# The gates' chain moved into its PSUM bank, and the join of the key halves' maxima made a one-operand reduction

## The reference

```python
x = x + tanh(g_xattn) * xattn(layernorm(x), ctx)        # 8 heads of 64, softmax, Wo, bo
x = x + tanh(g_ffn) * ffn(layernorm(x))

# ffn: attention of x with itself, 16 heads of 32 (q normalised, scaled, biased), giving h; then
gates = softmax(h @ Wr.T + br)                          # 15 routed gates per token
routed = gates * (one-hot mask of the 3 largest) * 3
sw = softmax(h @ Ws.T + bs)                             # 2 per token
shared = sw; weight_0 = sw * 2
masked = concat([weight_0[..., 0:1] * shared, weight_0[..., 1:2] * routed])
out = (h * masked.sum(-1, keepdims=True)) @ Wp.T + bp
```

## Time and profile before

| | us |
|---|---|
| median of 3 runs (lowest, highest) | 5000.62 (4998.94, 5014.54) |
| span of the profiled execution (its own device time is not listed apart) | 5005.2 |
| TensorE busy in it | 4571.6 (91%) |
| VectorE busy | 3138.7 (63%) |
| ScalarE busy | 2516.0 (50%) |
| GpSimd busy | 3389.9 (68%) |
| mean granted TensorE clock | 0.956 of full speed |

### The profile page before, as it was taken

The page is one execution under the profiler, slowest core; times in us unless marked ns, Lnnn a source line. Parts: engine busy times, 40 slices in busy tenths (PEclk is TensorE's granted clock), DMA queues, the critical chain, the costliest instruction groups (busy, mean ns, idle before and its releaser), DMA issues.

```text
span 5005.2 us, 67480 instructions
## 1 busy us (share of the span) xinstructions
PE 4571.6 (91%) x21568; PEld 2352.4 (47%) x21568; DVE 3138.7 (63%) x3955; ACT 2516.0 (50%) x4577; POOL 3389.9 (68%) x2667
## 2 busy tenths in 40 slices
PE   4899999999999999998989989999999899899886
PEld 3455555545454545454444544544444445444333
DVE  4554545454545454576767777776767677777764
ACT  3343434353434343445656656556556566465453
POOL 1665656565656565566777778777778687777766
PEclk8999999999999999999999999999999999999988
DMA  7466565756555656554344344353434353443432
GB/s 227 123 175 176 154 189 154 202 154 179 143 166 145 174 144 164 145 141 133 96 120 125 98 128 131 87 148 112 131 104 121 102 142 91 126 123 96 126 87 72
DMA packets 516174, 682.50 MB, mean 136 GB/s; under 512 B 42609, under 2 KB 371825, under 8 KB 506609
## 3 DMA queue, kind: packets, MB, share of 16 engines
q1 hardware_dynamic: 515824, 678.18, 48.9%
HBM read 323.83 MB, written 150.99 MB: 95 GB/s over the span
## 4 chain that ended last, share of the span: by engine, by line
PE 73%; DVE 10%; DMA 7%; issue 4%; ACT 4%; SPq 2%; POOL 1%; ACTq 0%; DVEq 0%; POOLq 0%
PE aux L903 25%; PE aux L995 19%; PE aux L1009 17%; PE aux L977 6%; DVE nm L1333 3%; PE aux L1021 3%; DVE h_raw L1353 2%; DMA xs<-x_after_xattn 2%; ACT probs L1193 1%; SPq L792 1%; DMA xs<-in_x 1%; DMA x_after_xattn<-xs 1%; PE aux L947 1%; DMA raw<-in_ctxT 1%; PE aux L1029 1%
## 5 line engine op out<-in xcount | busy, mean ns | idle before, releaser
L882 POOL TENSOR_TENSOR added<-added,probs 128x512 f32<-128x512 f32 x1433 | 1828.5, 1307 | 904.2 <-PE aux L1009 517.3
L1333 DVE TENSOR_REDUCE nm<-aux 128x2 f32<-128x1024 f32 x1536 | 1809.9, 1220 | 908.4 <-PE aux L977 907.5
L1193 ACT ACTIVATE probs<-aux 128x512 f32<-128x512 f32 x2151 | 1186.5, 599 | 1086.8 <-PE aux L995 1047.3
L995 PE MATMUL aux<-stack 128*128 128x512 f32 x4096 | 1430.0, 441 | 145.9 <-ACT probs L1193 61.6
L995 PEld LDWEIGHTS aux<-stack 128*128 128x128 f32 x4096 | 721.3, 193 | 1003.3 <-issue 340.4
L1009 PE MATMUL aux<-probs,v 128*32 128x512 f32 (+1 forms) x4302 | 985.2, 628 | 2.4 <-ACT probs L1193 1.3
L882 POOL TENSOR_TENSOR added_f<-added_f,probs 128x512 f32<-128x512 f32 x537 | 679.5, 1301 | 124.3 <-PE aux L1009 104.3
L977 PE MATMUL aux<-ck_hi,cq_hi 32*128 32x512 f32 (+1 forms) x3072 | 466.8, 499 | 167.9 <-DVE nm L1333 133.9
L903 PE MATMUL aux<-xT_hi,wqk 128*128 128x512 f32 x1536 | 584.1, 424 | 3.7 <-ACT v_out L1163 1.6
L977 PEld LDWEIGHTS aux<-ck_hi,cq_hi 32*128 32x128 f32 (+1 forms) x3072 | 183.8, 191 | 631.9 <-issue 607.3
L903 PE MATMUL aux<-wvo,parts 128*128 128x512 f32 x1536 | 406.6, 402 | 13.4 <-issue 9.6
(11 more groups left out here) (128 smaller groups left out, 4535.1 us busy)
## 6 DMA issues: line engine op xcount, KB each, us to landing
wqk<-w_split SPq DMA_DIRECT2D x256, 256.0 KB, 3.8
wvo<-w_split SPq DMA_DIRECT2D x64, 1024.0 KB, 7.2
parts<-h_kept SPq DMA_DIRECT2D x128, 512.0 KB, 4.2
stack<-cq_hi SPq DMA_DIRECT2D x128, 256.0 KB, 6.0
stack<-ck_hi SPq DMA_DIRECT2D x128, 256.0 KB, 6.4
v_kept<-v_out SPq DMA_DIRECT2D x128, 256.0 KB, 2.5
v<-v_kept SPq DMA_DIRECT2D x64, 512.0 KB, 6.1
h_kept<-h_hi SPq DMA_DIRECT2D x128, 256.0 KB, 2.4
```

Source lines behind the costliest of these rows:

```text
L882: pool.tensor_tensor(onto, onto, exp_buffer(T, e), ALU.add).then_inc(added_ok, 1)
L995: ins = pe.matmul(out, stack[:, g % 2, e * ph.SLOTS + ks, jt * P:(jt + 1) * P], stack[:, g % 2, e * ph.SLOTS + qs, n * HALF:(n + 1) * HALF ...
L1193: act.activation(exp_buffer(T, e), aux[:, o.bank["S", T, e], :], ACT.Exp, scale=ph.SCALE).then_inc(probs_ok, 1)
L1333: dve.tensor_reduce(nm[:, half, first:first + 2 * TT - t:TT], aux[:, b:b + 2, :], axis=AX.X, op=ALU.max, negate=True).then_inc(emptied["dv ...
```

## The change

The chain of the gates is no longer one item `gm` but three, `gs` (VectorE, up to the subtractions), `ge` (ScalarE, the exponential) and `gm` (VectorE, the rest), with planned times of 1, 0.2 and 2.6 us in place of `ga`'s 0.2 and `gm`'s 4 us, and due steps right after `gt`. The last half's logits are added in the gates' own PSUM bank, subtracted and exponentiated there, and sums live there too, so that no instruction of the chain has two tensor operands in SBUF; the bank is freed by `gm` rather than by `ga`. `gexp` falls away. `mc` becomes a reduction over the two halves' columns of `nm` into a new tensor `least`, which `mt` transposes. In `run`, the held rule is lifted where nothing is under way.

```diff
--- before.py
+++ after.py
@@ -118,7 +118,7 @@
 
 
 BATCH_HAS = {kind: n for n, kinds in (
-    (1, ("cl", "xl", "cx", "cxl", "ln", "la", "lb", "l2", "tr", "tra", "trl", "wv", "wo", "xr")), (2, ("gm",)),
+    (1, ("cl", "xl", "cx", "cxl", "ln", "la", "lb", "l2", "tr", "tra", "trl", "wv", "wo", "xr")), (2, ("gs", "ge", "gm")),
     (NG, ("wl", "pq", "pk", "pqa", "pka", "pql", "pkl", "ss", "ssa", "s2", "s3", "s3p", "sd", "mx", "mxr", "mc", "mt", "ml", "md", "vl")),
     (TT, ("vp", "vpe", "vs", "ol", "op", "ope", "xb", "st", "xq")), (HALVES, ("sm", "sma", "ev", "acc", "gt", "ga", "hs", "hsl", "hw")),
     (TURN, ("S", "ex", "ad", "PV"))) for kind in kinds}
@@ -219,7 +219,13 @@
                 self.add(("ev", h), "dve", 2.07, b + 0.6, [("sma", h), ("PV", T), ("ev", h - 1), ("hw", h - 1)])
                 if ph.ffn:
                     self.add(("gt", h), "pe", 0.45, b + 1, [("ev", h), ("fb", 0)])
-                    self.add(("ga", h), "dve", 0.2, b + 1.2, [("gt", h), ("gm", 2 * (h // HALVES - 1) + h % 2)])
+                    if h // 2 % NG < NG - 1:
+                        self.add(("ga", h), "dve", 0.2, b + 1.2, [("gt", h)])
+                    else:
+                        part = 2 * (h // HALVES) + h % 2
+                        self.add(("gs", part), "dve", 1, b + 1.2, [("gt", h)])
+                        self.add(("ge", part), "act", 0.2, b + 1.3, [("gs", part)])
+                        self.add(("gm", part), "dve", 2.6, b + 1.4, [("ge", part), ("ope", TT * j - 1)])
                 self.add(("hs", h), "act", 0.55, b + 1, [("ev", h)])
                 self.add(("hsl", h), "dve", 0.6, b + 1.2, [("hs", h), ("gt", h)])
                 self.add(("hw", h), "sp", 1.3, b + 1.5, [("hsl", h)])
@@ -326,9 +332,6 @@
         last = [("vp", TT * (j + 2) - 1, whole - 1)] if j + 1 < 2 * B else [("op", TT * j - 1, NG - 1)]
         self.add(("wo", j), "sp", 1.3, b0 + at["out"][0] - 4, last + [("ws", ph.W + 3)])
         self.add(("xr", j), "sp", 2.6, b0 + at["xr"], [("tr", j + 1, 1, NG - 1), ("st", TT * j - 1), ("fs", NG * j + NG - 1)])
-        if ph.ffn:
-            for half in range(2):
-                self.add(("gm", 2 * j + half), "dve", 4, b0 + (2 if half else -4), [("ga", HALVES * (j + 1) - 2 + half), ("ope", TT * j - 1)])
         for i in range(TT):
             half, t = i // (TT // 2), TT * j + i
             b = b0 + at["out"][0] + at["out"][1] * i
@@ -379,7 +382,7 @@
                     engine, time, _ = work[it]
                     unit = Order.unit(it)
                     if it[0] in Order.TAKER and unit not in banks:
-                        if held and it[0] not in ("S", "PV", "sm", "gt"):
+                        if held and events and it[0] not in ("S", "PV", "sm", "gt"):
                             continue
                         b = some(it[0], 4 if it[0] == "mx" else 1)
                         if b is None:
@@ -467,6 +470,8 @@
             return [(("mxr", *unit[1:], p), banks[2 * p:2 * p + 2]) for p in range(2)]
         if unit[0] == "acc":
             return [(("ev", unit[1]), banks)]
+        if unit[0] == "gt" and unit[1] // 2 % NG == NG - 1:
+            return [(("gm", 2 * (unit[1] // HALVES) + unit[1] % 2), banks)]
         kind = "pqa" if unit[0] == "pq" and stage(batch(unit)).ffn else Order.TAKER[unit[0]]
         return [((kind,) + unit[1:], banks)]
 
@@ -498,10 +503,10 @@
         xs = sb("xs", [P, TT // 2, DM])
         xT_hi = sb("xT_hi", [P, NG, N], F32R)
         xT_lo = sb("xT_lo", [P, NG, N], F32R)
-        qb, sq, qy, more, bv, bo_f, blk, wg, top, glog, gexp, gsum, added_f = earlier(
+        qb, sq, qy, more, bv, bo_f, blk, wg, top, glog, gsum, added_f = earlier(
             ("qb", [P, 2, HALF], F32), ("sq", [P, HALF], F32), ("qy", [P, HALF], F32), ("more", [P, F.NP - X.NP, HALF], F32), ("bv", [P, DM], F32),
             ("bo_f", [P, DM], F32), ("blk", [P, P], F32), ("wg", [P, NG, GC], F32), ("top", [P, TT // 2, 8], F32),
-            ("glog", [P, 2, TT // 2, GC], F32), ("gexp", [P, TT // 2, GC], F32), ("gsum", [P, 3, TT // 2], F32), ("added_f", [P, 4, HALF], F32))
+            ("glog", [P, 2, TT // 2, GC], F32), ("gsum", [P, 2, TT // 2], F32), ("added_f", [P, 4, HALF], F32))
         kv_hi = sb("kv_hi", [P, KC, N], F32R)
         kv_lo = sb("kv_lo", [P, KC, N], F32R)
         raw = sb("raw", [P, N])
@@ -521,6 +526,7 @@
         v = sb("v", [P, 2, TT, P])
         parts = sb("parts", [P, 2, 2, NG, P], F32R)
         nm = sb("nm", [P, 2, F.G * TT])
+        least = sb("least", [P, F.G * TT])
         mrow = sb("mrow", [F.G * TT, P], F32R)
         ident = sb("ident", [P, P])
         ones = sb("ones", [P, X.SUM])
@@ -608,6 +614,10 @@
             (taker, _), = o.takers(unit, [])
             wait_drained(eng, [taker])
 
+        def last_gates(part):
+
+            return HALVES * (part // 2) + HALVES - 2 + part % 2
+
         def last_maxima(g):
 
             return ("mx", g, stage(g // NG).UNITS - 1)
@@ -980,7 +990,7 @@
                         out = bank(it)
 
                         pe.wait_ge(maxima_ok, it[1] + 1)
-                        done(it, pe.transpose(out[0:G * TT, 0:P], nm[:, 0, 0:G * TT], ident[:]))
+                        done(it, pe.transpose(out[0:G * TT, 0:P], least[:, 0:G * TT], ident[:]))
                     elif kind == "S":
                         _, T, e = it
                         g, s = divmod(T, STEPS)
@@ -1204,9 +1214,10 @@
 
                         wait_emptied(act, ("sm", h))
                         act.activation(h_hi[:], h_raw[:], ACT.Copy).then_inc(h_hi_ok, 1)
-                    elif kind == "gm":
+                    elif kind == "ge":
                         act.wait_ge(gates_in, it[1] + 1 - 2 * B)
-                        act.activation(gexp[:], glog[:, it[1] % 2], ACT.Exp).then_inc(gates_exp, 1)
+                        logits = aux[:, o.bank["gt", last_gates(it[1])], 0:TT // 2 * GC]
+                        act.activation(logits, logits, ACT.Exp).then_inc(gates_exp, 1)
 
             @block.vector
             def _(dve):
@@ -1335,7 +1346,10 @@
                     elif kind == "mc":
                         g = it[1]
                         wait_drained(dve, [("mxr", g, ph.UNITS - 1, p) for p in range(2)])
-                        dve.tensor_tensor(nm[:, 0, 0:G * TT], nm[:, 0, 0:G * TT], nm[:, 1, 0:G * TT], ALU.min).then_inc(maxima_ok, 1)
+                        if g:
+
+                            wait_emptied(dve, ("mt", g - 1))
+                        dve.tensor_reduce(least[:, 0:G * TT], nm[:, :, 0:G * TT].rearrange("p h t -> p t h"), axis=AX.X, op=ALU.min).then_inc(maxima_ok, 1)
                     elif kind == "ml":
                         g = it[1]
                         src = full(("mt", g))
@@ -1372,37 +1386,46 @@
 
                             wait_emptied(dve, ("gt", h - 2))
                         dve.tensor_tensor(glog[:, h % 2], src, before, ALU.add).then_inc(emptied["dve"], 1)
-                    elif kind == "gm":
-                        part = it[1]
-                        first = part % 2 * TT // 2
-                        lg, eg = glog[:, part % 2], gexp[:]
-                        kept, share, both = (gsum[:, i, :] for i in range(3))
-                        wait_emptied(dve, ("gt", 4 * part + 6 if part % 2 == 0 else 4 * part + 3))
+                    elif kind == "gs":
+                        h = last_gates(it[1])
+                        lg = full(("gt", h))[:, 0:TT // 2 * GC].rearrange("p (t c) -> p t c", c=GC)
+
+                        wait_emptied(dve, ("gt", h - 2))
+                        link(dve.tensor_tensor(lg, lg, glog[:, h % 2], ALU.add))
                         dve.tensor_reduce(gm[:, :, 0], lg[:, :, 0:NE], axis=AX.X, op=ALU.max)
                         link(dve.tensor_reduce(gm[:, :, 1], lg[:, :, SH:SH + 2], axis=AX.X, op=ALU.max))
                         dve.tensor_tensor(lg[:, :, 0:NE], lg[:, :, 0:NE], gm[:, :, 0:1].to_broadcast([P, TT // 2, NE]), ALU.subtract)
                         dve.tensor_tensor(lg[:, :, SH:SH + 2], lg[:, :, SH:SH + 2], gm[:, :, 1:2].to_broadcast([P, TT // 2, 2]), ALU.subtract).then_inc(gates_in, 1)
+                    elif kind == "gm":
+                        part = it[1]
+                        first = part % 2 * TT // 2
+                        held = aux[:, o.bank["gt", last_gates(part)], :]
+                        eg = held[:, 0:TT // 2 * GC].rearrange("p (t c) -> p t c", c=GC)
+                        kept, both = (held[:, (TT // 2 * GC + i * TT // 2):(TT // 2 * GC + (i + 1) * TT // 2)] for i in range(2))
+                        share = gsum[:].rearrange("p i t -> p t i")
                         dve.wait_ge(gates_exp, part + 1 - 2 * B)
                         for t in range(TT // 2):
                             dve.max(top[:, t, :], eg[:, t, 0:NE])
                         dve.tensor_reduce(g1[:, 0], eg[:, :, 0:NE], axis=AX.X, op=ALU.add)
```

(20 more changed lines are left out.)

## The result

The changed kernel takes 4944.6 us in the median of four runs (4937.9 to 4957.6), the kernel before, in four runs, 5007.6 (4998.9 to 5015.1). The ratio is 0.9877, 95% interval 0.9858 to 0.9896: 61.6 us less (52 to 71) by the 5000 us on which the prediction stands. That is faster, as forecast, and inside the range of 4865 to 4965, but 40 us short of the forecast's own 101, in the band of "partly given back".

A forecast was written before the change was run, and what follows sets the result against it. TensorE, 91% busy, was taken to bound the kernel, standing still in the second half for VectorE's contended gates' chain. Terms -83.7 - 32.5 + 8 + 8 + 1 - 2 = -101 us gave 4900 us, range 4865 to 4965.

The forecast's parts named there:

- partly given back: Rival: bank, slack and order costs come together, or TensorE often stays at the lower clock; 4935 to 4970 us, chance 0.18.
- What bounds, and the gates' gaps: Second half: fourteen TensorE gaps behind the gates' chain go, -83.7 us; clock regained, -32.5; slack after stalls lost, +8.
- The operands: VectorE's gates' chain: one PSUM operand per two-tensor instruction avoids GpSimd contention; a part takes 3.3 us, not 11.7.
- The join: Maxima's join mc as a one-operand reduction frees 37 us of VectorE but saves 2 us; bounds 0 and -10.
- The new order: Order placed anew behind the first gate part, after 2550 us: taken at 0, bounds +-32 us.
- the bank: Gates' PSUM bank held 3.8 us longer per part: 8 us cost, bounds nothing and 27 us.
- gs ahead of hsl: VectorE takes the first gates item before the low half of h, delaying the last output product: +1 us.
- The new order costs more than the gaps: Rival: maxima matmuls without free bank pairs hold products behind them, costing 131 us; then 5020 us, slower chance 0.05.

The follow-up runs named there:

- experiment 3: Kernel before, order untouched, the nine two-SBUF instructions of each gates' part replaced by one-operand reductions (gate products left out): 4889.6 us, ratio 0.9782.
- experiment 4: Changed kernel's plan and order, with the gates computed in SBUF as before: 5052.7 us, ratio 1.0103.
- experiment 1: Changed kernel with hsl (the low half of h) issued on GpSimd instead of VectorE, same order: 4882.8 us, ratio 0.9768.
- experiment 11: Kernel before, old order, with one-operand stand-ins in the gates' chain (products left out), hsl on GpSimd and the one-operand maxima join: 4863.9 us, ratio 0.9709.
- experiment 2: Kernel before with hsl issued on GpSimd at its place, nothing else: 4992.4 us, ratio 0.9982.
- experiment 5: Kernel before with only the maxima's join made a one-operand reduction into a new tensor: 4987.5 us, ratio 0.9971.
- experiment 12: Changed kernel with the old two-SBUF-operand join of the maxima: 4984.0 us, ratio 0.9958.
- experiment 9: Changed kernel with hsl issued ahead of ga or gs where it stood right behind it on VectorE: 4978.2 us, ratio 0.9967.
- experiment 8: Changed kernel with hsl as four instructions of 128 columns, still on VectorE: 5143.7 us, ratio 1.0285.

## Why the prediction was right in sign and short in size

- **What bounds, and the gates' gaps** (-83.7, -32.5, +8, together -108): right. At an unchanged order it measured -109, and its trace has 90 us less idle and 30 us less busy for about the same work (experiment 3): the clock came back with the gaps.
- **The operands**: right to the row, as every step of the chain shows. The old arithmetic in the new plan is 52 us slower than before (experiment 4), the new one 62 us faster. The 65 ns that the Trainium skill (VectorE: DVE Perf Modes, the section on the TRN2 errata) gives a PSUM source do not show: L1397 takes 229 ns where the uncontended L1383 took 223, L1398 165 against L1384's 161, and a reduction that reads PSUM and writes SBUF (L1395) 221 where the one from SBUF (L1381) took 200.
- **The join** (-2 us, bounds 0 and -10): mis-sized. It measured -14.5 at the old order and -40 at the new one. I had counted only TensorE's direct waits for it, 3.7 us. VectorE works in order, so a microsecond less there moves everything behind it, hsl too, against GpSimd's additions, for the better or, as with the hsl at 2421.82 us, for the worse. How much of the 14.5 and 40 is that, the runs do not separate.
- **The new order** (0, bounds +-32) and **the bank** (+8): the step that failed. Against 109 + 14.5 = 123.5 us for the two edits at the old order, the change brought 61.6: the new order cost 62 us, where 9 were in the sum (8 for the bank, 1 for gs ahead of hsl). With hsl off VectorE that cost is 29.5 us (experiments 1 and 11), inside the bounds for bank and order. The other 32 (with an uncertainty of some 24, as five ratios enter) are hsl. More directly: to take hsl off VectorE gains 54.5 us at the new order, and 9 to 22 at the old (experiment 2; experiment 11 against 3 and 5). The counts agree: hsl of 7 us and more stand four, four and five times in the traces of the old order (before, experiments 3 and 5), nine, eight and ten times in those of the new one (after, experiments 4 and 12). I had shown the line once, uncontended (L1353 in the earlier trace rows), and priced no wait for it: I took only the gates' instructions for contended, and never looked at that line's longest, 35.4 us, in the trace of before. The bank's share of the 29.5 was not taken apart; no wait of TensorE for its release shows.
- **gs ahead of hsl** (+1 us at the end): overtaken by the 25.9 us hsl near the end.
- **The rivals**: "partly given back" came true in size (its 4935 to 4970 holds 4944.6) but not in mechanism: the clock did come back in part (0.97), no wait for the bank shows, and the time was lost behind hsl. "The new order costs more than the gaps" names the right place, but half of its 131 us was measured, and the held rule is not shown as the cause.
- **Luck**: that the time lies inside the range owes something to errors of opposite sign. The new order cost 53 us more than the sum had for it, and the join gave 38 us more at that order. Without the join the changed kernel stands at 0.9958, some 4979 us, outside the range (experiment 12).

Still open: what decides whether a two-SBUF instruction gets in after one GpSimd addition or has to wait until GpSimd pauses. Of 128 hsl in the changed kernel 119 got in after at most one addition, 81 of them although GpSimd, counted from the start of the hsl, ran on for over 7 us. Neither size nor neighbour decides, and the pair at 2425.82 and 2421.82 us shows that a place in the order does not either. Nor was it tried to keep hsl on VectorE with an operand in PSUM.

## What to carry to other kernels

An instruction with two SBUF operands on VectorE beside a busy GpSimd has a price that its own duration does not show: look at the most, not at the median, of each such line, and count its waits again whenever its place moves. Remove the whole class, not the nearest member: the changed kernel cured the gates and left hsl. Where the order is planned from assumed times, measure an edit at the old order first; here that separated 109 us of gain from some 62 us that the new order cost.

## What the runs showed of the hardware

- A waiting VectorE instruction gets in behind the GpSimd instruction then under way, or else only when GpSimd pauses; nothing between was seen. In the seven traces that have all 128 undivided hsl on VectorE (before, after, experiments 3, 4, 5, 9 and 12), 844 of 896 take at most 1.9 us and 52 take 7.0 to 35.5 us, and each of the 52 ends 0.55 us after the last of a run of GpSimd instructions without a gap: 25.9 us through 21 of them, 35.4 (the kernel before) through 29. The Trainium skill, SBUF — State Buffer, section Who interferes with whom, calls the port pair that the two engines share an exclusive lock, and says of VectorE's two-port modes that whoever issues first has it for the whole instruction and the other blocks fully. The traces agree for one instruction and show that the loser can lose again many times.
- Consecutive two-SBUF instructions mostly take turns with GpSimd (experiment 8): 1.36 us in the median for a second, third or fourth quarter of 128 columns, against 0.28 us for a quarter and 0.68 us for all 512 columns uncontended.
- TensorE's granted clock in the 6 us behind a gate gap was 0.61 of full speed in the mean, between its two levels of 1.2 and 2.4 GHz. Over 2550 to 4750 us it was 0.96 in the kernel before, and 0.98 without those gaps (experiment 3).
